# A two-stage mixture kernel on one core: unit samples loaded as 64-column blocks and turned by VectorE instead of transposed by TensorE

## What is computed

```python
def dense(x, wi, wo): return relu(x @ wi) @ wo          # 256 -> 1024 -> 256
s0, s1 = dense(x, swi[0], swo[0]), dense(x, swi[1], swo[1])   # two shared networks
eo = dense(x, wi[label], wo[label])                     # the sample's own, one of five
w  = softmax(relu(concat(eo[:,0], s0[:,0], s1[:,0]) @ g1) @ g2)
x  = x + eo*w0 + s0*w1 + s1*w2
x  = x + zX*lap_x(x) + zY*lap_y(x) + zR*x*(1-x)         # finite differences over tokens, features
```

## Time and profile before

| | |
|---|---|
| median of three executions | 1137.41 us |
| profiled execution | 1138.1 us, span 1136.6 us |
| granted TensorE clock | 1.00 of full speed |
| TensorE (PE), weight loads (PEld) | 99%, 85% of the span |
| VectorE (DVE), ScalarE (ACT), GpSimd (POOL) | 59%, 40%, 7% |
| DMA | 111.82 MB, 98 GB/s on average |

### The profile page before, as it was taken

One profiled execution on the slowest core, in us unless ns is written; L12 is line 12 of the kernel. 1 busy time (PEld: TensorE's weight loads), 2 busy tenths in 40 slices (PEclk: granted clock), 3 DMA queues, 4 the chain that ended last, 5 costly groups with the idle time before them and its releaser, 6 DMA issues.

```text
span 1136.6 us, 16584 instructions
## 1 busy us (share of the span) xinstructions
PE 1129.7 (99%) x5956; PEld 962.7 (85%) x5956; DVE 674.2 (59%) x1007; ACT 456.3 (40%) x790; POOL 78.8 (7%) x123
## 2 busy tenths in 40 slices
PE   9999999999999999999999999999999999999998
PEld 8888888888888888888888888888888888888888
DVE  5665667666666635556646555555566465555556
ACT  2554556565565522333333323333333333233233
POOL 1211212111121000000000000000000000000001
PEclk9999999999999999999999999999999999999999
DMA  8555656556665413113023022121130230220200
GB/s 269 174 162 177 190 182 199 180 181 181 177 204 163 115 44 97 24 61 84 19 66 85 11 74 48 47 75 28 58 84 18 66 84 14 72 62 33 75 29 24
DMA packets 111251, 111.82 MB, mean 98 GB/s; under 512 B 78441, under 2 KB 87234, under 8 KB 111170
## 3 DMA queue, kind: packets, MB, share of 16 engines
q1 hardware_dynamic: 96706, 59.58, 19.3%
q0 software_dynamic: 13952, 50.60, 14.8%
q10 hardware_dynamic: 512, 0.59, 0.2%
HBM read 89.40 MB, written 17.04 MB: 94 GB/s over the span
## 4 chain that ended last, share of the span: by engine, by line
PE 96%; DVE 1%; SPq 1%; DMA 1%; issue 0%; ACT 0%; DVEq 0%; ACTq 0%
PE acc L1033 30%; PE hbank L964 15%; PE hbank L965 15%; PE hbank L966 15%; PE acc L1034 15%; SPq L1384 1%; PE tbank L912 1%; PE acc L1019 1%; PE acc L1002 1%; PE hbank L937 0%; DMA rw<-in_L_cond_swi 0%; PE hbank L938 0%; PE acc L1003 0%; PE hbank L980 0%; PE hbank L981 0%
## 5 line engine op out<-in xcount | busy, mean ns | idle before, releaser
L643 DVE SCALAR_TENSOR_TENSOR hl<-hbank,hh 128x512 fp32r<-128x512 f32 (+1 forms) x416 | 271.6, 654 | 410.6 <-ACT hh L1144 410.1
L1144 ACT ACTIVATE hh<-hbank 128x512 fp32r<-128x512 f32 (+1 forms) x416 | 235.7, 568 | 560.3 <-PE hbank L966 557.0
L1033 PE MATMUL acc<-swo,hh 128*128 128x512 f32 x992 | 359.3, 396 | 0.0
L1034 PE MATMUL acc<-swo,hl 128*128 128x256 f32 x992 | 277.8, 280 | 0.0
L1033 PEld LDWEIGHTS acc<-swo,hh 128*128 128x128 f32 x992 | 186.3, 188 | 43.7
L964 PE MATMUL hbank<-xh,swh 128*128 128x512 f32 (+1 forms) x528 | 205.3, 389 | 0.0
L965 PE MATMUL hbank<-xl,swh 128*128 128x512 f32 (+1 forms) x528 | 205.0, 388 | 0.0
L966 PE MATMUL hbank<-xh,swl 128*128 128x512 f32 (+1 forms) x528 | 202.1, 383 | 0.0
L1034 PEld LDWEIGHTS acc<-swo,hl 128*128 128x128 f32 x992 | 187.1, 189 | 9.6
L1033 PE MATMUL acc<-ewo,hh 128*128 128x512 f32 x496 | 180.0, 395 | 0.3 <-DVE hl L643 0.3
L1034 PE MATMUL acc<-ewo,hl 128*128 128x256 f32 x496 | 139.0, 280 | 0.0
(11 more groups left out here) (209 smaller groups left out, 972.4 us busy)
## 6 DMA issues: line engine op xcount, KB each, us to landing
rw<-in_L_cond_wi POOLq DMA_DIRECT2D x44, 512.0 KB, 4.5
rw<-in_L_cond_wo POOLq DMA_DIRECT2D x44, 512.0 KB, 4.8
eo_scratch<-eo SPq DMA_DIRECT2D x128, 64.0 KB, 2.2
xs<-in_x SPq DMA_DIRECT2D x16, 512.0 KB, 4.3
rw<-in_x SPq DMA_DIRECT2D x256, 32.0 KB, 2.2
ei<-eo_scratch SPq DMA_DIRECT2D x16, 512.0 KB, 5.5
xs<-in_x SPq DMA_DIRECT2D x125, 64.0 KB, 3.5
out<-ot SPq DMA_DIRECT2D x15, 512.0 KB, 6.3
```

The costliest lines, as they stand in the source:

```text
L643: e.scalar_tensor_tensor(h_slot(HL, g), bank[:, 0:w], 0.0, h_slot(HH, g).bitcast(F32), ALU.max, ALU.subtract).then_inc(h_lo, 1)
L1033: e.matmul(acc[j][:, 0:2 * D], HH[:, g % NH, js], woc[:, c, :], start=(c == 0), stop=False)
L1034: m = e.matmul(acc[j][:, D:2 * D], HL[:, g % NH, js], woc[:, c, 0:D], start=False, stop=last)
L1144: e.activation(h_slot(HU if upright(g) else HH, g), hbank[g % HRING][:, 0:w], ACT.Relu).then_inc(h_hi, 1)
```

## The change

All units but the first are loaded as blocks and turned by VectorE, as the shared tiles are. A sample's load takes runs of 64 features: row 32a + t/2 of `xs` gets tokens t and t+1 of the features 64a to 64a+63. A 32 by 32 transpose into `xz` (a buffer of its own now) gives, on row 32a + r, the features 64a + r and 64a + 32 + r; so the features are split into these two halves, and the rows of the first-layer weights are loaded to match, in two issues per piece. The token order in a tile is now even tokens, then odd tokens, of each sample in turn; the results' rows are stored in that order (even_odd). The first unit is still transposed by TensorE, from rows in that same order. The shared tiles' blocks are loaded in 4 issues of 128 KB in place of 16. `hh` and `hl` have three places, with a fourth (`hhx`, `hlx`) for the last two chunks; some weight cuts move to other chunks. VectorE's turn, ScalarE's copy and VectorE's subtraction for the next tile stand at chunks 2, 3 and 6 or 7 of the pass before (earlier or later around units of two samples).

```diff
-NH = 4
+NH = 3
+NHF = 4
...
+TURN, HIGH, LOW = {}, {}, {}
+for _n in range(2, 1 + NU):
+    if tiny(_n):
+        continue
+    _tile = tile_of(_n) + 1
+    if _n == 2:
+        _at = (4, 5, 7)
+    else:
+        _at = (2, 3, 5 if tiny(_n + 1) else 7 if blocks(_n) == 4 else 6)
+    TURN[_n, _at[0]] = HIGH[_n, _at[1]] = LOW[_n, _at[2]] = _tile
+    if tiny(_n + 1):
+        TURN[_n, 6] = HIGH[_n + 1, 0] = LOW[_n + 1, 0] = _tile + 1
...
-            at = {0: (n + 1, 2)}
+            at = {2: (n + 1, 2)}
...
-            at = {1: (n + 1, 0), 2: (n + 1, 2), 4: (n + 1, 1), 5: (n + 1, 3), 7: (n + 2, 0)}
+            at = {1: (n + 1, 0), 2: (n + 1, 2), 5: (n + 1, 1), 6: (n + 1, 3), 7: (n + 2, 0)}
+        elif blocks(n) == 2:
+            at = {2: (n + 1, 0), 4: (n + 1, 2)}
...
+        def turned_cols(a, k):
+            return a[:].rearrange("p (q k i) -> p k q i", k=2, i=32)[:, k, :, :]
...
+        def sample_blocks(v, tile, b):
+            return (flat(XS[tile % 2])[:, 128 * b:128 * b + 128],
+                    x[bass.ds(v, 1), :, :].rearrange("z t (a d) -> (z a) t d", d=64))
+        def sample_rows(a, b):
+            return a[64 * (b % 2):64 * (b % 2) + 64, b // 2, :]
+        def even_odd(a, v):
+            return a[bass.ds(v, 1), :, :].rearrange("z (i h) d -> (z h) i d", h=2)
...
+        def piece_loads(to, a, b, p, plain=False):
...
+                a = a.rearrange("z (a k e) f -> k (z a) e f", k=2, e=32)
+                return [(to[:, k, :], a[k][:, :, p * 512:(p + 1) * 512]) for k in range(2)]
...
+            def turn_tile(tile):
+                if tile > 2:
+                    e.wait_ge(xt_lo, turned(tile - 1))
+                if tile <= NU:
+                    w = 128 * UNITS[tile - 1][1]
+                    e.wait_ge(x_in[tile % 2], X_VAL[tile])
+                    e.transpose(XZ[:, 0:w], flat(XS[tile % 2])[:, 0:w]).then_inc(xz_done, 1)
+                    return
...
# SP, load_unit_x and store_unit
-                if tile >= 3:
-                    e.wait_ge(t_prod, T_AT[tile_last(tile - 2)])
+                if tile == 3:
+                    e.wait_ge(t_prod, T_AT[1, 1])
+                if tile > 3:
+                    e.wait_ge(xz_done, turned(tile - 2))
...
-                    e.dma_start(XS[tile % 2][b:128:k, 0:k // 2, :],
-                                x[bass.ds(v, 1), :, :].rearrange("a (p j) d -> (a p) j d", p=128 // k)) \
-                        .then_inc(x_in[tile % 2], 16)
+                    to, src = (sample_rows(XS[1], b), even_odd(x, v)) if tile == 1 else sample_blocks(v, tile, b)
+                    e.dma_start(to, src).then_inc(x_in[tile % 2], 16)
...
-                    e.dma_start(eo_d[bass.ds(v, 1), :, :].rearrange("a (p j) d -> (a p) j d", p=128 // k),
-                                EO[u % 2][b:128:k, 0:k // 2, :]).then_inc(eo_out[u % 2], 16)
+                    e.dma_start(even_odd(eo_d, v), sample_rows(EO[u % 2], b)).then_inc(eo_out[u % 2], 16)
...
# SP, load_tile_blocks
-                    for a in range(4):
-                        e.dma_start(to[32 * a:32 * a + 32, :, 32 * q:32 * q + 32],
-                                    rows[:, :, 32 * a:32 * a + 32]).then_inc(xb_in[t % 2], 16)
+                    rows = x[8 * t + 2 * q:8 * t + 2 * q + 2, :, :].rearrange("b t (a d) -> a (b t) d", d=64)
+                    e.dma_start(to[:, q, :, :], rows).then_inc(xb_in[t % 2], 16)
```

More of the change, by code:

```diff
@@ L106, in tile_parts @@
 def tile_parts(n, c):
[L108 to L121, removed]
+    return [(1, 0), (1, 1)] if (n, c) == (1, 7) else []
 T_ORDER = ["counts"]
@@ L139, with turned @@
 T_AT = {key: i + 1 for i, key in enumerate(T_ORDER)}
[L140 to L153, removed]
+TURN, HIGH, LOW = {}, {}, {}
[10 more added lines that the diff above has]
+        TURN[_n, 6] = HIGH[_n + 1, 0] = LOW[_n + 1, 0] = _tile + 1
+for _t in range(NT):
+    _n, _c = (FIRST - 1, 6) if _t == 0 else (FIRST + 2 * _t - 1, 4)
+    TURN[_n, _c] = HIGH[_n, _c] = LOW[_n, _c + 1] = 1 + NU + _t
+def turned(tile):
+    return tile - 1
 LAST_PASS = {tile_of(n): n for n in range(NP)}
-def tile_last(tile):
-    return (tile, 1) if (tile, 1) in T_AT else (tile, None)
 SHARED_PIECES = [(ws, p) for ws in range(2) for p in range(4)]
@@ L186, in unit_cuts @@
             out.append(at[c])
-    if 3 <= n <= 1 + NU and tiny(n - 1) and c < 2:
+    if 3 <= n <= 1 + NU and blocks(n - 1) < 4 and c < 2:
         out.append((n, 1 + 2 * c))
@@ L428, in bank_free @@
             return (h_hi, g + 1 - 2 * NC) if upright(g) else low_done(g)
-        def tile_bank(tile, k):
-            return acc[2 + k] if tile == 1 else tbank
         def inner(t):
@@ L782, in _ @@
                     for tile, k in tile_parts(n, c):
[L783 to L787, removed]
+                        first_low(k)
+                    if (n, c) in LOW:
+                        tile_low(LOW[n, c])
+                    if (n, c) in TURN:
+                        turn_tile(TURN[n, c])
                 if (n, c) == (2, 5):
@@ L832, in _ @@
                         add_x_last(0)
-                if g < G and not tiny(n):
+                if g < G:
                     for ws, p in low_parts_at(n, c):
@@ L946, in first_product @@
                 wh, wl, _ = weights(n)
[L947 to L951, removed]
-                else:
-                    js = slice(HALVES[n][0], 4, 2) if n in HALVES else slice(0, 4)
-                    xh, xl = ([tile_cols(a[tile % 2], k)[:, js, :] for k in range(2)] for a in (XH, XL))
-                    to = bank[:, 0:w].rearrange("p (j n) -> p j n", n=128)
-                    if c == 0:
-                        e.wait_ge(xt_lo, PASSES[n][1] // 2 + 1)
+                if n in HALVES:
+                    js = slice(HALVES[n][0], 4, 2)
+                    xh, xl = ([turned_cols(a[tile % 2], k).rearrange("p (j q) i -> p j q i", j=4)[:, js, :, :]
+                               for k in range(2)] for a in (XH, XL))
+                    to = bank[:, 0:w].rearrange("p (j q i) -> p j q i", q=4, i=32)
+                else:
+                    xh, xl = ([turned_cols(a[tile % 2], k)[:, 0:w // 32, :] for k in range(2)] for a in (XH, XL))
+                    to = bank[:, 0:w].rearrange("p (q i) -> p q i", i=32)
+                if c == 0 and tile > 1:
+                    e.wait_ge(xt_lo, turned(tile))
                 if c % 4 == 0:
@@ L1063, in _ @@
                     for tile, k in tile_parts(n, c):
-                        transposes(tile, k)
+                        first_transposes(k)
                 if (n, c) == (2, 5):
```

171 lines of the change are left out of this document (77 added, 94 removed).

## The result

The changed kernel takes **1299.09 us** (median; 1294.87 to 1306.67) against 1137.63 of the kernel before on the same chip: a ratio of 1.143 [1.137, 1.148]. The forecast was 1236 us, 99 more than before; 161 more came, which is just inside the upper end of the range. The profiled execution took 1300.03 us, its span is 1298.5. The kind was right (transfers of the unit stage, TensorE idle behind them), the size was not, and two further places lost time.

A forecast was written before the change was run, and what follows sets the result against it. TensorE bound the kernel before; after the change the busiest DMA engine bounds the unit stage at 510 us, ending it 100 us late, TensorE's 15.1 us worth nothing: 1138.1 + 99 = 1237, so 1236 us, range 1120 to 1300.

The forecast's parts named there:

- TensorE's saving: Unit stage: 124 transposes, 13.5 us, and 1.6 us of waits for the transposed bank leave TensorE's path, together 15.1 us.
- The kind of loss: Unit stage: narrow issues load few DMA engines, so samples and result places come late and TensorE idles some 100 us.
- the busiest engine's work in the unit stage: Stores, first unit, blocks and weights on the busiest DMA engine sum to 483 to 573 us, taken as 510, against 410.
- POOL issues two more transfers per unit; nothing: POOL's queue: two more transfers per unit were priced at nothing, as POOL is busy 7%.
- its rule on the outermost count: DMA issues are cut along the outermost count, taken as the smaller of both sides, 2 or 4, on the same engines.
- Rival 3: First products on TensorE: sixteen 32-value runs cost up to 4 ns each, 8 us come back, 1131 us; chance 0.03.
- the shared stage keeps its length: Shared stage after the units: its transfers need some 10 us per tile against over 40, so its length stays.
- Rival 2: Unit stage: only the loads are narrow, the stage fits, TensorE stops once at the start, 1131 us; chance 0.05.
- The first unit's samples: Start of the unit stage, in rival 2 alone: samples come some 5 to 10 us late and stop TensorE once.
- Rival 1: Unit stage: narrow issues spread over the engines, under 0.7 busy, so TensorE is the bound again, 1123 us; chance 0.20.
- The clock: Granted clock, 1.00 before, may fall where TensorE idles; in a stage bound by transfers that adds little.

The follow-up runs named there:

- E12: E8 with the edits of E9 and E10, and GpSimd issues the fourth unit's odd samples ahead of the third unit's weights: 1137.96 us, ratio 1.000.
- E2: The changed kernel with each block load as four issues of 32 rows, one per 64 columns, stores unchanged: 1412.09 us, ratio 1.242.
- E3: The changed kernel with the same narrow block loads issued by GpSimd from the third unit on, behind the weights: 1227.17 us, ratio 1.081.
- E6: The changed kernel with the same issues, but only 16 of 128 rows in each weight issue from the third unit on: 1194.25 us, ratio 1.049.
- E5: The changed kernel with each first-layer weight piece of the units in one issue with 128 rows outermost, as before: 1248.45 us, ratio 1.098.
- E9: E8 with x's high and low parts written half by half, so first products read 512 values in one run: 1145.98 us, ratio 1.007.
- E0: Not a run: what is fetched once the last unit's results have landed, ending the unit stage; at 423.45 us before the change, 575.64 after.
- E7: The changed kernel with each store as two issues of 32 rows and each first-layer weight piece as four of 32 rows: 1209.00 us, ratio 1.063.
- E10: E8 with each of the first unit's eight samples loaded as two issues of 32 rows instead of one of 64: 1147.22 us, ratio 1.007.
- E8: E7 with GpSimd issuing every second sample of a unit, from the third unit on, between its weights: 1158.62 us, ratio 1.020.
- E4: The changed kernel with SP loading a unit's registers in a row, then issuing its loads or stores in a row: 1288.57 us, ratio 1.132.

## Why the prediction went wrong

- **TensorE's saving, 15.1 us: right.** E12's profiled execution shows 14.6 with no gap in the units. In after it is worth nothing, as forecast.
- **The kind of loss: right in its outcome, wrong in its server.** Narrow stores and loads did lengthen the unit stage, through the turn and the evacuation, and the DMA share did fall. They are also cut as the prediction took it: from 75 to 520 us SP's queue carries 630 packets of 4 bytes beside 108 stores and 103 block loads, and 2 x 108 + 4 x 103 are 628. But the step "the busiest engine's work in the unit stage", taken as 510 us, names the wrong resource: E2 and E3 change the time by +113 and -72 us against that sum. The server is SP: the prediction counted packets on engines and gave no price to the instruction that issues them. A sample's load and store together kept SP for 2.0 us before (256 us for 128 of each) and for 4.1 after. E6 puts SP's own pace at 44 us over the 410 that the stage took before, and what it loses beside weights at 108. That the sum of 510 lies near the 562 us of the stage is luck.
- **"POOL issues two more transfers per unit; nothing": the term that was mis-sized.** E5 measured 51 us, and 63 us were missing in the forecast; without them the loss is 111 us, where the forecast has 99, near for the wrong reason. The prediction applied its rule on the outermost count to samples and stores, and not to the first-layer pieces, whose count had also gone to four. Had the pieces been on the same four engines always, that rule would have added 21 x 192 KB to each of the four, some 190 us at the 21.8 GB/s of the earlier trace rows, where E5 shows 51. The Trainium skill, "DMA: Bandwidth & Descriptors", section "Why a DMA increments its semaphore by 16 and not by 1", lets issues of GpSimd move round the engines; no run here shows which they took.
- **Rival 3, short runs: it held, beside the forecast.** The forecast took zero from equal mean durations at one run and at four and gave it 0.03. Sixteen runs were in no row of before; with them the mean durations rise by 6, 3 and 11 ns, and E9 measured 9.6 us in the shared stage, near the rival's own price of 8. It also falsifies "the shared stage keeps its length": from E0's fetch to the end it took 722.9 us instead of 713.1.
- **Rival 2, only the loads narrow**, was built in E7, with the weights wide too: 1209.00 us and not 1131, since the narrow loads, all on SP, still bring E0 56 us later than before.
- **The first unit's samples** were priced at 5 to 10 us in rival 2 alone. They cost 12.2 us of waiting, and E10 got 11 us back where TensorE sets the pace again; in after, where SP does, no run shows what they cost. The forecast's sum left them out.
- **Rival 1 as a value**, 1123 us with TensorE bound, was sound: E12's profiled execution took 1128.31, with a start 3.5 us later and 1.1 us more after the units than before. Its reason, issues that spread by themselves, did not hold: stores and weights had to be cut wide and the narrow loads shared between two queues.
- **The clock** "adds little": not so small. From first to last unit product TensorE is 132 us later and idle for 112.4 of them; with the 14.6 saved, some 34 us are products that ran slower, at a granted clock of 0.88; the mean of the second products is 425 ns instead of 395 (396 in E8, at 0.99). As SP, with only 20 us of waiting, set the stage's end, this slowness lay beside its work and cost nothing further.

## What to carry to other kernels

When loads and stores are re-cut, price the queue that issues them as an engine of its own: instructions times their duration, plus what they wait for their own issues ahead and for another queue's large packets; a queue that waited 140 of 410 us had room for 1.5 times its work, not for twice. A rule about shapes has to be applied to every transfer whose shape the change touches, also to those on another queue that look like bookkeeping. And equal times for one run and for four say nothing of sixteen: where an operand changes its layout, the price has to be measured at the layout that the change brings.

## What the runs showed of the hardware that was not expected

- A register load on SP takes some 270 ns behind a 16-wide issue and some 740 ns behind one with 2 or 4 outermost (medians 267 and 742); read in a row it takes 272, and the next narrow issue waits instead (E4).
- An issue's price on SP follows its shape: 315 ns for 32 rows of 1 KB, 564 ns for 32 rows of two 256-byte runs, and the same for all four quarters (E2); GpSimd takes 1.33 us for a block load (E3).
- Beside 4 KB packets of another queue SP's queue, of 256-byte and 1 KB packets, falls from 45 to 12 GB/s; with an eighth of their bytes the same stage is 108 us shorter (E6).
- A moving operand in 16 runs of 32 values costs TensorE 3 to 9 ns of 221 to 226 per matmul from start to start, and its mean durations rise by 3 to 11 ns of 389 to 396 (E8 against E9).
